# One product of four moved from VectorE to GpSimd, and products added in pairs by accumulating transfers, in a state-space and mixture-of-experts kernel

## The reference, cut to what matters

```
x = setup: 32 batches x 512 positions x 256 features
xn = layernorm(x)
delta, B, C = split(xn @ W_deltaBC.T)            # 64, 16 and 16 wide
delta = softplus(delta @ W_dt.T + b_dt)          # [b, 512, 256]
for each of the 16 states n:
    h_n[t] = exp(delta[t] * A_n) * h_n[t-1] + delta[t] * xn[t] * B_n[t]
y = sum over n of h_n * C_n  +  D * xn
ffn = for each of 8 experts: take the 128 positions of a batch with the highest softmax,
      gelu(rows @ W1 + b1) @ W2 + b2, times the gate, added back to those positions
out = x + y + ffn
```

## Time and profile before

| | us |
|---|---|
| median of 3 runs | 2570.74 (2570.37 to 2574.43) |
| the profiled execution's own time | 2570.78 |
| its span, first to last instruction | 2569.1 |
| busy: PE | 2362.7 (92%) |
| busy: VectorE | 2429.4 (95%) |
| busy: ScalarE | 1958.2 (76%) |
| busy: GpSimd | 2200.3 (86%) |

### The profile page before, as it was taken

One profiled execution on the slowest core, in us unless ns is written; L12 is line 12 of the kernel. 1 busy time (PEld: TensorE's weight loads), 2 busy tenths in 40 slices (PEclk: granted clock), 3 DMA queues, 4 the chain that ended last, 5 costly groups with the idle time before them and its releaser, 6 DMA issues. The chain is left out here.

```text
span 2569.1 us, 32727 instructions
## 1 busy us (share of the span) xinstructions
PE 2362.7 (92%) x10412; PEld 1776.6 (69%) x10412; DVE 2429.4 (95%) x2092; ACT 1958.2 (76%) x3436; POOL 2200.3 (86%) x1258
## 2 busy tenths in 40 slices
PE   6747999999989999999999999999999999999996
PEld 2315777777767777777777777777777777777775
DVE  5599999999989999999999999999999999999995
ACT  6646787878777878787778788777777878777783
POOL 4325999989989999999999899899988899999996
PEclk9968999999999999999999999999999999999998
DMA  9983455344544444444444444444445344354343
GB/s 338 366 309 122 130 169 143 108 125 98 136 99 136 105 135 101 124 109 110 133 113 129 111 110 125 100 131 116 129 96 144 99 119 121 93 148 99 88 103 54
DMA packets 143768, 342.10 MB, mean 133 GB/s; under 512 B 16784, under 2 KB 101872, under 8 KB 126960
## 3 DMA queue, kind: packets, MB, share of 16 engines
q1 hardware_dynamic: 71728, 239.11, 26.3%
q0 software_dynamic: 70656, 100.70, 21.6%
q10 hardware_dynamic: 1216, 0.23, 0.0%
HBM read 251.89 MB, written 101.71 MB: 138 GB/s over the span
## 5 line engine op out<-in xcount | busy, mean ns | idle before, releaser
L481 POOL TENSOR_TENSOR ysum<-ysum,prod 128x1024 f32<-128x1024 f32 x480 | 1297.8, 2704 | 96.9 <-DVE prod L898 93.7
L889 DVE TENSOR_TENSOR_SCAN bank_x<-decay,bank_x 128x1024 f32<-128x1024 f32 x512 | 1169.8, 2285 | 0.0
L1079 PE MATMUL bank_l<-ext,w_sb 128*128 128x256 f32 x4096 | 965.1, 382 | 29.4 <-ACT og L668 19.6
L1095 PE MATMUL bank_l<-w_sb,hid 128*128 128x256 f32 x4096 | 991.2, 393 | 0.0
L1079 PEld LDWEIGHTS bank_l<-ext,w_sb 128*128 128x128 f32 x4096 | 758.8, 191 | 191.5 <-ACT og L668 32.4
L1095 PEld LDWEIGHTS bank_l<-w_sb,hid 128*128 128x128 f32 x4096 | 767.5, 193 | 162.4 <-issue 38.8
L832 DVE TENSOR_TENSOR bank_x<-du,bank_b 128x1024 f32<-128x1024 f32 x512 | 617.8, 1207 | 55.2 <-PE bank_b L994 55.2
L625 ACT ACTIVATE hid<-bank_l,b_all 128x256 f32<-128x256 f32 x1024 | 430.6, 475 | 295.5 <-PE bank_l L1079 294.9
L616 ACT ACTIVATE decay<-delta,a_sb 128x511 f32<-128x511 f32 x1024 | 640.0, 707 | 1.2
L898 DVE TENSOR_TENSOR prod<-bank_x,c_all 128x1024 f32<-128x1024 f32 x512 | 621.8, 1214 | 0.1
L500 POOL DMA_INDIRECT out<-og,idx_all x256 | 409.3, 1599 | 49.1 <-POOL ysum L481 37.3
(11 more groups left out here) (94 smaller groups left out, 1646.5 us busy)
## 6 DMA issues: line engine op xcount, KB each, us to landing
c_all<-c_rows SPq DMA_DIRECT2D x128, 1024.0 KB, 5.4
w_sb<-in_w SPq DMA_DIRECT2D x32, 1024.0 KB, 8.9
decay<-in_x SPq DMA_DIRECT2D x32, 512.0 KB, 6.5
xn_rows<-decay POOLq DMA_DIRECT2D x32, 512.0 KB, 5.9
xn_cols<-delta SPq DMA_DIRECT2D x32, 512.0 KB, 5.5
xnt<-xn_cols SPq DMA_DIRECT2D x32, 512.0 KB, 6.7
out<-yrow POOLq DMA_DIRECT2D x32, 512.0 KB, 7.1
ex<-xn_rows,idx_all POOLq DMA_INDIRECT x256, 2.8
```

Source lines behind the costliest of these rows:

```text
L481: nc.gpsimd.tensor_tensor(ysum[:, m % 2], first, prod[:, i], ALU.add).then_inc(sum_done, 1)
L889: nc.vector.tensor_tensor_scan(bank_x[:, s % 2], decay[:, k % 2, i].rearrange("p c t -> p (c t)"), bank_x[:, s % 2], 0.0, ALU.mult, ALU.ad ...
L1079: i = nc.tensor.matmul(bank_l[(q + k) % 2][:, (f % 2) * UT:(f % 2 + 1) * UT], w1_sb[:, e2, hc, f * P:(f + 1) * P], ext[:, k % 2, hc], star ...
L1095: i = nc.tensor.matmul(o, hid[:, (k - 1) % 2, f, c * K:(c + 1) * K], w2_sb[:, le2, f], start=False, stop=(f == FC - 1))
```

## The change

State 0 of each unit's four is handled differently. Its scan writes to a new SBUF tile `state`, and GpSimd multiplies it with C (`multiply_c`), so VectorE does three products a unit in place of four. The four products are no longer added one by one: product 0 is added onto product 1, and product 3 onto product 2, by accumulating transfers within SBUF of 512 KB each that GpSimd issues (`merge_pair`), and GpSimd adds the two sums to `ysum` (`add_pair`). GpSimd's order within a unit is new. The making of the middle part of B on ScalarE moves from the middle of unit 1 to the end of its unit 1, and SP moves the three parts in units 1, 2 and 3 in place of one after the other in unit 1; `take_lo` goes to unit 2. TensorE's two bias matmuls of 256 columns a unit become one of 512.

```
-                    for i in range(STEPS):
-                            pool.wait_ge(prod_done, s + 1)
-                            nc.gpsimd.tensor_tensor(ysum[:, m % 2], first, prod[:, i], ALU.add).then_inc(sum_done, 1)
...
+            def multiply_c(u):
+                pool.wait_ge(scan_done, u * STEPS + 1)
+                pool.wait_ge(c_in[u % 2], (u // 2 + 1) * 16)
+                wait(pool, pair_in[0], u * 16)
+                nc.gpsimd.tensor_tensor(prod[:, 0], state[:], c_all[:, u % 2, 0][:, None, :].broadcast_to([P, HC, T]),
+                                        ALU.mult).then_inc(pool_prod_done, 1)
+            def merge_pair(u, pair):
+                pool.wait_ge(prod_done, dve_prods(u * STEPS + 2 * pair + 2))
+                if pair == 0:
+                    pool.wait_ge(pool_prod_done, u + 1)
+                    pool.dma_start(prod[:, 1], prod[:, 0], accum_op=ALU.add).then_inc(pair_in[0], 16)
+                else:
+                    pool.dma_start(prod[:, 2], prod[:, 3], accum_op=ALU.add).then_inc(pair_in[1], 16)
+            def add_pair(u, pair):
+                pool.wait_ge(pair_in[pair], u * 16 + 16)
...
+                nc.gpsimd.tensor_tensor(ysum[:, b % 2], first, prod[:, 1 + pair], ALU.add).then_inc(sum_done, 1)
...
+                    if there(u - 1, NU):
+                        merge_pair(u - 1, 1)
+                    if sl == 3 and there(b, NB) and there(b + 1, NB):
+                        take_delta(b + 2, (m + 1) % 2)
+                        take_du(b + 2, (m + 1) % 2, (j * 2 + (m + 1) // 2 + 1) * 16)
+                    if sl == 1 and there(b, NB) and there(b + 1, NB):
+                        take_rest(b + 2)
+                    if there(u + 2, NU):
+                        gather(u + 2)
+                    if there(u, NU):
+                        multiply_c(u)
+                    if there(u - 2, NU):
+                        scatter(u - 2, 0)
+                    if there(u - 1, NU):
+                        add_pair(u - 1, 1)
+                    if there(u, NU):
+                        merge_pair(u, 0)
+                    if there(u - 2, NU):
+                        scatter(u - 2, 1)
+                    if sl == 2 and there(b, NB) and there(b + 1, NB):
+                        take_lo(b + 2)
+                    if sl == 0 and there(b - 2, NB):
+                        add_y(b - 2, u)
+                    if there(u, NU):
+                        add_pair(u, 0)
...
-                        if pair == 1 and sl == 1 and there(b, NB) and there(b + 1, NB):
-                            take_mid(b + 2)
...
                         if sl == 1:
+                            take_mid(b + 2)
                             take_z(b + 2, (m + 1) % 2, 0)
...
+                        if i == 0:
+                            wait(dve, pool_prod_done, u)
+                            into = state[:].rearrange("p c t -> p (c t)")
+                        else:
+                            into = bank_x[:, s % 2]
+                        nc.vector.tensor_tensor_scan(into, decay[:, k % 2, i].rearrange("p c t -> p (c t)"),
                                                      bank_x[:, s % 2], 0.0, ALU.mult, ALU.add).then_inc(scan_done, 1)
                         if there(s + 1, NB * N):
                             multiply_b(s + 1, par if n < N - 1 else 1 - par, b if n < N - 1 else b + 1)
                         if i == 0:
+                            continue
+                        if i == 1:
                             dve.wait_ge(c_in[u % 2], (u // 2 + 1) * 16)
-                        wait(dve, sum_done, s - 3)
+                            wait(dve, sum_done, u * 2 - 1)
+                        if i == 2:
+                            wait(dve, sum_done, u * 2)
+                        if i == 3:
+                            wait(dve, pair_in[1], u * 16)
                         dve.wait_ge(scan_done, s + 1)
                         nc.vector.tensor_tensor(prod[:, i], bank_x[:, s % 2].rearrange("p (c t) -> p c t", c=HC),
```

More of the change, by code:

```diff
@@ L115, in build @@
         c_all = sb("c_all", [P, 2, STEPS, T])
+        state = sb("state", [P, HC, T])
         prod = sb("prod", [P, 4, HC, T])
@@ L234, in build @@
         prod_done = sem("prod_done")
+        pool_prod_done = sem("pool_prod_done")
+        pair_in = [sem(f"pair_in{i}") for i in range(2)]
         sum_done = sem("sum_done")
@@ L265, in batch_of, with dve_prods @@
             return u // 64 * HALF + u % 8 * UB + i
+        def dve_prods(s):
+            return s // STEPS * (STEPS - 1) + max(s % STEPS - 1, 0)
         def expert_of(u):
@@ L336, in move_parts, with move_mid, move_low @@
                 sp.dma_start(bcs[0:32, par], bc_hi[64:96, :]).then_inc(hi_moved, 16)
+            def move_mid(nb, par):
                 held(mid_done, nb)
                 sp.dma_start(bcs[32:64, par], bc_mid[64:96, :]).then_inc(mid_moved, 16)
+            def move_low(nb, par):
                 held(lo_done, nb)
@@ L344, in load_c @@
                 held(c_out, (u // SLOTS + 1) * 16)
-                held(prod_done, (u - 1) * STEPS)
+                held(prod_done, dve_prods((u - 1) * STEPS))
+                held(pool_prod_done, u - 1)
                 first = u % SLOTS * STEPS
@@ L348, in load_c @@
                              .broadcast_to([P, STEPS, T])).then_inc(c_in[u % 2], 16)
-            move_parts(1, 0, 0)
+            move_high(1, 0, 0)
+            move_mid(1, 0)
+            move_low(1, 0)
             load_c(0)
@@ L363, in main @@
                     if sl == 1 and there(b + 1, NB):
-                        move_parts(b + 2, (m + 1) % 2, b * N)
+                        move_high(b + 2, (m + 1) % 2, b * N)
+                    if sl == 2 and there(b + 1, NB):
+                        move_mid(b + 2, (m + 1) % 2)
+                    if sl == 3 and there(b + 1, NB):
+                        move_low(b + 2, (m + 1) % 2)
                     if sl != 0:
@@ new lines, in add_pair @@
+            def add_pair(u, pair):
+                b, n = u // SLOTS, u % SLOTS * STEPS + 2 * pair
+                pool.wait_ge(pair_in[pair], u * 16 + 16)
+                if n == 0:
+                    pool.wait_ge(skip_done, b + 1)
+                    wait(pool, y_tr, b * 2 - 2)
+                    first = skip[:]
+                else:
+                    pool.wait_ge(sum_done, u * 2 + pair)
+                    first = ysum[:, b % 2]
+                nc.gpsimd.tensor_tensor(ysum[:, b % 2], first, prod[:, 1 + pair], ALU.add).then_inc(sum_done, 1)
@@ new lines, in scatter @@
+            def scatter(w, c):
+                pool.wait_ge(og_done, w * UB + UB)
+                wait(pool, scattered[w % 2][c], w // 2 * 16)
+                if batch_of(w, c) in y_before:
+                    pool.wait_ge(y_added, 16 * (batch_of(w, c) + 1))
+                pool.indirect_dma_start(
+                    out=out_rows,
+                    out_offset=bass.IndirectOffsetOnAxis(ap=idx_all[:, w * UB + c:w * UB + c + 1], axis=0),
+                    in_=og[:, w % 2, c], in_offset=None, compute_op=ALU.add,
+                ).then_inc(scattered[w % 2][c], 16)
@@ L461, in main, with add_y @@
+            def add_y(y, u):
+                pool.wait_ge(yrow_done, y * 2 + 2)
+                wait(pool, y_added, 16 * y)
+                last = [w for w in range(min(u - 1, NU)) for c in range(UB) if batch_of(w, c) == y]
+                if last:
+                    pool.wait_ge(scattered[last[-1] % 2][y % UB], (last[-1] // 2 + 1) * 16)
+                y_before[y] = True
+                pool.dma_start(out_tiles[y], yrow[:], accum_op=ALU.add).then_inc(y_added, 16)
             def main(j):
@@ L468, in main @@
                         pool.wait_ge(resid_out[1], 16 * HALF // UB)
-                    for i in range(STEPS):
-                        n = sl * STEPS + i
-                        s = b * N + n
-                        if there(b, NB):
-                            pool.wait_ge(prod_done, s + 1)
[L474 to L480, removed]
-                            nc.gpsimd.tensor_tensor(ysum[:, m % 2], first, prod[:, i], ALU.add).then_inc(sum_done, 1)
[L482 to L513, removed]
@@ new lines, in main @@
+                    if there(u - 1, NU):
+                        merge_pair(u - 1, 1)
+                    if sl == 3 and there(b, NB) and there(b + 1, NB):
+                        take_delta(b + 2, (m + 1) % 2)
+                        wait(pool, bx_done, b * N)
+                        take_du(b + 2, (m + 1) % 2, (j * 2 + (m + 1) // 2 + 1) * 16)
[3 more added lines that the diff above has]
+                        gather(u + 2)
@@ L830, in multiply_b @@
                 dve.wait_ge(du_done, b + 1)
-                wait(dve, prod_done, s - 1)
+                if s % STEPS == 2:
+                    wait(dve, scan_done, s - 1)
+                else:
+                    wait(dve, prod_done, dve_prods(s - 1))
```

(9 more changed lines are left out.)

8 lines of the change are left out of this document (4 added, 4 removed).

## The result

The changed kernel takes 2746.6 us (median of 4, 2744.5 to 2750.6) against 2570.6 for the kernel before: ratio 1.068, 95% interval 1.066 to 1.070. Forecast were 2793 us, between 2610 and 2970, and slower. The main loop went from 72.9 us a batch to 78.3 (2507 us for 32 batches, 204 to 2711 us).

The account below looks back on a forecast made before the run. GpSimd's in-order queue was to bound the kernel: 61.1 us of program, 11.6 of issues and 7.75 of waits make 80.45 us a batch against 73.5. Over 32 batches that adds 222 us to 2570.8, 2793 us, range 2610 to 2970.

Parts of the forecast that it names:

- Which engine sets the end: Main loop: VectorE first before, TensorE and GpSimd within 4 us; after the change GpSimd's queue with visible waits is last.
- GpSimd's elementwise work: GpSimd's queue: four elementwise operations fewer at 2.4 us each, 9.6 us a batch off 70.7, leaving 61.1.
- The issue: GpSimd's queue: eight accumulating-transfer issues a batch at 1.45 us a slot, 11.6 us, with bounds of 0.96 and 1.54.
- The landing of pair 0: GpSimd's addition of pair 0: the transfer lands 4.4 us after its issue, costing 7.75 us of waits a batch.
- No waits for pair 1: GpSimd's addition of pair 1: 6.6 us of work between issue and use covers the landing in all but the worst case.
- VectorE's part: VectorE: drops to about 67 us a batch; most of its 13 us idle is before step 2's product, for GpSimd's addition.
- The scan into SBUF: VectorE's scan of state 0: writing SBUF in place of PSUM makes no difference to its 2.29 us.
- The dependent scan: VectorE, scan of step 1 right behind the B product it reads: costs 0.12 us a unit more.
- TensorE's, ScalarE's and SP's parts: Moved B part, bias matmuls and SP moves: TensorE near 69 us a batch, moves free, gains not cashed if GpSimd is slower.
- The hidden transfers: Rival: cheap issues and early landings hide the transfers, GpSimd needs 70.8 us a batch, 2499 us; chance 0.11.
- Transfers as slow as y's: Rival: transfers land after 6.0 us at 1.54 us a slot, 87.55 us a batch, 3020 us; chance 0.05.
- The chain back to product 2: Within the hidden-transfers rival: VectorE's last product through GpSimd to step 2's product and on takes 20.4 us in unit 3.

Follow-up runs that it names:

- Run 2: The changed kernel with the middle part of B, its moves and the bias matmuls put back as before, only products and sums changed: 2741.8 us.
- run 9: The changed kernel with gathers after pair 0's issue, C load held until pair 1 lands, GpSimd multiplying only in units 0 and 2: 2484.1 us.
- run 8: The changed kernel with accumulating transfers of 256 KB, the other half of products 0 and 3 left out of the sum: 2620.0 us.
- run 4: The changed kernel with SP holding each unit's 1 MB C load until the transfer of pair 1 has landed: 2694.7 us.
- run 5: The changed kernel with two buffers for product 2 and the C load held until pair 1 has landed: 2684.8 us.
- Run 7: The changed kernel with GpSimd's two gathers after pair 0's issue and the C load held until pair 1 has landed: 2564.1 us.

## Why the prediction was right, step by step

**Which engine sets the end.** Right. Three engines lie within 4 us, and the one that the change loads is not the one that it relieves. Run 2 shows that gains elsewhere aren't cashed, run 9 that they are when GpSimd has room.

**GpSimd's elementwise work**, 9.6 us off 70.7: right. With eight slots of 1.0 us, 61.1 + 8.0 = 69.1 was due, and 69.5 was measured.

**The issue** was mis-sized: 1.45 us a slot taken, 1.0 measured, 3.6 us a batch too much. The term took accumulation as a fixed price on top of a plain issue of 0.79. Here the accumulating issue is 0.9 us, against 1.37 for y's, and it stays 0.9 when the length of the 128 rows, and so the bytes, is halved (run 8). So it is neither a fixed price nor a matter of bytes. Two differences from y's issue are left, a quarter of the rows and a target in SBUF in place of HBM; no run parts them. The slot lay near the low bound of 0.96.

**The landing of pair 0** was mis-sized too: L = 4.4 was taken and 3.6 measured, 4.4 us a batch of waits for 7.75. The straight line of run 8 gives 1.1 fixed and 1.25 for each 256 KB, where the working had 1.3 and 1.5. That the bytes cost more than a plain load's fits a sum read from both places (512 KB of the C load were 1.5 us of the engines, these 2.5), but no run shows the reason.

**No waits for pair 1** is the step that failed. "6.6 us, enough in every case below but the worst" compared the cover with a landing by itself. 3.8 us a batch are spent there. The prediction did ask about the C load, but only for pair 0, where it is long over; the product that frees it is also the one that pair 1 needs. Runs 4 and 5 show it: with the load held the waits are gone and pair 1 lands in 4.5 us for 8.8.

**Luck in the number and in its sign.** The two oversized terms, 3.6 us of issues and 3.35 of pair 0's waits, are together the 6.95 us by which the forecast lay above the old 73.5. With both as measured the prediction's sum is 61.1 + 8.0 + 4.4 = 73.5, no change at all. What makes the kernel slower is what the sum had at nothing: pair 1's 3.8 us, with 0.5 of small waits and 0.4 more of GpSimd's own program, 78.2 of the 78.3. The sum of 80.45 missed 78.3 by 2.2, 70 us in 32 batches, and the time by only 46, mostly because it compared with 73.5 in 600 to 1500 us, where the mean of the whole main loop was 72.9. So the mechanism (GpSimd's queue with its waits is last) was right, and that it came out inside the range leans on errors that offset each other.

**VectorE's part.** The scan into SBUF costs nothing: 2276 ns for 2288. The idle time stands where it was expected, before the product, for GpSimd's additions: 114.3 / 11.5 = 9.9 us a batch, forecast "most of its 13". The dependent scan begins 0.1 us after its predecessor's end (1215.75 to 1215.85), 0.2 us later than an independent one, for 0.12. TensorE's, ScalarE's and SP's parts have no visible cost: run 2, without them, is within 5 us.

**The rivals.** The hidden transfers: not here. Run 7 comes near that case, and it gives 2564 us, not 2499. Its waits for transfers are the 2.0 us a batch that the rival named; it is GpSimd's program, 69.5 for 68.8, and 0.9 of other waits that make 72.4 out of 70.8. Transfers as slow as y's: true for pair 1 alone. The chain back to product 2 isn't the bound: run 5, with it loosened, is within 0.5% of run 4.

The Trainium skill ("DMA: Bandwidth & Descriptors", the anatomy of one DMA on the GpSimd path) fits a transfer as 2.0 us plus its bytes at 436 GB/s, by which an estimate is 3.2 us for 512 KB and 2.6 for 256. Here 512 KB alone landed 3.6 us after the end of the issue and 256 KB 2.4 us. So the fit is near in size, but between these two sizes the bytes go at half its rate (256 KB in 1.25 us, 210 GB/s).

## What to carry to other kernels

An operation replaced by a transfer costs its issue plus whatever its landing outlasts the work placed between, in an in-order queue; count that work for each transfer by name. Then ask what other transfer the same event releases: here a transfer of 512 KB with 6.6 us of cover was late because one of 1 MB left at the same moment, and taking away an engine's wait moved that collision to a transfer with less cover. When engines are within a few per cent of each other, move only as much as the receiving one has room for: beside the moved middle part alone (-2.5%), half the multiplications gave -3.4%, all of them -0.3% at best. And when a forecast comes out, redo its sum with the measured terms: this one, so corrected, said that nothing would change.

## What was not expected of the hardware

A second buffer made the kernel 11% slower (3047 us for 2747), and one wait on SP that keeps the C load off pair 0 took all of it back (2685 us). An accumulating transfer of 512 KB within SBUF landed 4.5 to 5.6 us after the start of its issue where nothing large ran beside it, and 6.4 to 11.9 beside a load of 1 MB. GpSimd issued it in 0.9 us (128 rows of 4 KB), against 1.37 for y's 512 KB (512 rows of 1 KB, to HBM); with 128 rows of 2 KB it was 0.9 us too.
